# Row transposes issued singly between the relus, two more units turned straight from SBUF, and weight splits that begin six units earlier, in a one-core kernel of attention and a mixture of experts

## The reference

```python
def ref(x, ...):                      # x: (4, 1024, 256) float32
    xn = layernorm(x)
    s = attention(xn)                 # 8 heads of 128, one shared K and V, causal; Wo at the end
    g = silu(moe(xn))                 # 8 experts, top 2 of a router, softmax gates
    return x + s * g

def moe(x):
    logits = x @ router_w + router_b
    gating = softmax(only_top_2(logits))
    h = relu(x @ w1[e] + b1[e])       # for each expert e: 256 -> 1024
    y = h @ w2[e] + b2[e]             # 1024 -> 256
    return sum over e of y * gating[:, e]
```

## Time and profile before

| | us |
|---|---|
| median of three runs | 1049.65 |
| lowest, highest | 1047.79, 1051.46 |
| the profiled execution | 1046.62 |
| its span, first to last instruction | 1044.80 |
| PE busy in the span | 983.1 (94%) |
| VectorE (DVE) busy | 856.7 (82%) |
| ScalarE (ACT) busy | 641.7 (61%) |
| GpSimd (POOL) busy | 333.9 (32%) |
| mean granted clock of PE | 0.997 of full speed |

### The profile page before, as it was taken

How to read it: one execution, slowest core, us unless ns; L and a number is a source line. 1 busy time by engine, 2 the same in 40 slices (tenths; PEclk the granted TensorE clock), 3 DMA queues, 4 the chain that set the end, 5 groups by cost and what they waited for, 6 DMA issues and landing times.

```text
span 1044.8 us, 25199 instructions
## 1 busy us (share of the span) xinstructions
PE 983.1 (94%) x8422; PEld 763.7 (73%) x8422; DVE 856.7 (82%) x1700; ACT 641.7 (61%) x1382; POOL 333.9 (32%) x342
## 2 busy tenths in 40 slices
PE   0798999999999999998999999999999999999997
PEld 0566888888888898885666667676776776777776
DVE  7895587787765546458999999999999999999972
ACT  3843332333332334336989889898888888888860
POOL 2014999899997300002101101212122111212111
PEclk9999999999999999999999999999999999999999
DMA  8978667778766522217999999999999999999993
GB/s 282 250 284 174 176 192 188 201 183 199 177 174 174 146 47 63 61 37 177 166 183 189 167 180 169 197 190 172 190 189 180 185 182 181 180 170 167 173 174 101
DMA packets 428269, 179.44 MB, mean 172 GB/s; under 512 B 363850, under 2 KB 417940, under 8 KB 427380
## 3 DMA queue, kind: packets, MB, share of 16 engines
q1 hardware_dynamic: 364416, 131.75, 61.6%
q10 hardware_dynamic: 57252, 28.38, 12.2%
q0 software_dynamic: 6480, 17.70, 7.3%
HBM read 54.94 MB, written 34.87 MB: 86 GB/s over the span
## 4 chain that ended last, share of the span: by engine, by line
PE 35%; DVE 14%; issue 2%; DMA 1%; ACT 1%; SPq 1%; DVEq 0%; ACTq 0%
PE b_psS L1376 11%; PE b_psO L1404 11%; PE b_psJ L1421 6%; DVE b_ph L1617 5%; PE b_psJ L1335 5%; DVE b_nmax L1579 4%; PE b_psS L1432 2%; PE b_psO L1407 1%; DVE b_outs L1623 1%; DVE b_psJ L1587 1%; DVE b_Q L1601 1%; DMA b_pT<-b_ph 1%; DVE b_psS L1577 0%; DVE b_f L1629 0%; ACT b_pr L1486 0%
## 5 line engine op out<-in xcount | busy, mean ns | idle before, releaser
L1036 PE MATMUL psU<-bxT,w_p 128*128 128x256 f16 (+1 forms) x1920 | 287.4, 261 | 9.0 <-DMA bxT<-expert_rows 3.0
L1127 ACT ACTIVATE h<-psU,bias 128x256 f32<-128x256 f32 (+1 forms) x320 | 123.7, 448 | 255.2 <-PE psU L1036 182.9
L1045 PE MATMUL psY<-w_p,hp 128*128 x1704 | 274.7, 274 | 0.6 <-DVE hp L1157 0.6
L1486 ACT ACTIVATE b_pr<-b_psS,b_nmax 128x1024 f32<-128x1024 f32 (+7 forms) x256 | 188.0, 742 | 55.5 <-DVE b_nmax L1577 36.0
L1376 PE MATMUL b_psS<-b_kp,b_Q 128*128 128x512 f16 (+3 forms) x1152 | 215.2, 326 | 2.6 <-PEq L1216 1.5
L1036 PEld LDWEIGHTS psU<-bxT,w_p 128*128 x1920 | 187.3, 98 | 31.9 <-issue 13.2
L1404 PE MATMUL b_psO<-b_pT,b_vp 128*128 128x256 f16 x1536 | 202.9, 273 | 5.2 <-issue 3.4
L1617 DVE SCALAR_TENSOR_TENSOR b_ph<-b_pr,b_rrec,b_ph 128x1024 f16<-128x1024 f32 (+7 forms) x256 | 199.1, 809 | 1.8 <-ACT b_ph L1516 1.8
L1155 DVE CAST hp<-h 128x512 f16<-128x512 f32 (+1 forms) x160 | 91.7, 573 | 126.7 <-ACT h L1127 112.6
L1516 ACT ACTIVATE b_ph<-b_pr,b_rrec 128x1024 f16<-128x1024 f32 (+7 forms) x256 | 187.9, 779 | 0.0
L1045 PEld LDWEIGHTS psY<-w_p,hp 128*128 128x128 f16 x1704 | 166.5, 98 | 22.2 <-issue 1.4
(11 more groups left out here) (197 smaller groups left out, 1060.2 us busy)
## 6 DMA issues: line engine op xcount, KB each, us to landing
wstage<-in_L_ffn_w SPq DMA_DIRECT2D x48, 256.0 KB
expert_rows<-rowx SPq DMA_DIRECT2D x67, 128.0 KB
expert_outputs<-y ACTq DMA_DIRECT2D x31, 256.0 KB
b_pT<-b_ph SPq DMA_TRANSPOSE x320
a_x_all<-in_L_attn_x SPq DMA_DIRECT2D x8, 512.0 KB, 8.9
a_w_raw<-in_L_ffn_w SPq DMA_DIRECT2D x4, 1024.0 KB, 9.1
xn_split<-a_xp SPq DMA_DIRECT2D x4, 1024.0 KB, 9.0
xn_turned<-a_xT SPq DMA_DIRECT2D x3, 1024.0 KB, 16.1
```

The lines of the kernel that those rows point to most:

```text
L1036: mm = eng.matmul(psU[w % U][:, g % 2, 0:tiles * P].rearrange("p (t r) -> p t r", t=tiles), weight(n, a * W1 + c * H + g * P, P), bxT[n % ...
L1045: mm = eng.matmul(psY[n % 2][:, t, :], hp[n % 2][:, a, g, t * P:(t + 1) * P], weight(n, 2 * W1 + (2 * g + b) * D, D), start=(g == 0 and k ...
L1127: a = eng.activation(h32[w % 4][:, g, 0:rows], psU[w % U][:, g, 0:rows], ACT.Relu, bias=bias[:, ds(e * HT + 2 * q + g, 1)], scale=1.0 / WS)
L1486: a = eng.activation(pr[k % 3][:, o:o + w], psS[BUF[i]][:, :, :].rearrange("p a n -> p (a n)")[:, o:o + w], ACT.Exp, bias=nmax[:, at:at + ...
```

## The change

- The number of units that are turned straight becomes six: 4 and 5 join. Their two row buffers lie in the second buffer of `hp`, which block 1 is the first to fill, so VectorE waits before its first split of block 1 for both transposes. The four ring buffers go on with unit 6. GpSimd's gathers of units 4 and 5 still wait for the straight transposes of 0 and 1.
- ScalarE's transposes: `load(n, t)` issues one. In block n the first one for block n + 2 stands between the second and the third relu pair, the second one (if that block is a twin) between the third and the fourth; the read of the number of expert n + 1 stands there too. The first waits for the stores of its unit, as before, and for the straight transposes of units 4 and 5.
- VectorE reads the expert's number for its addition at the block's start, before its first split.
- GpSimd gathers 4 and 5, and from unit 6 on alternates gather and split. SP, too, alternates store and load of weights from unit 6 on, and b2's broadcast stands before the store of unit 8.

```diff
--- before.py
+++ after.py
@@ -137,7 +137,9 @@
     moe = Arena(nc, late_at)
     wstage = [moe.take(f"wstage{i}", [P, 512], F32) for i in range(2)]
     pe16 = Arena(nc, moe.at).take("a_pe16", [P, 2, T], F16)
-    rowx = [moe.take(f"rowx{i}", [P, 2 * D], F16) for i in range(4)]
+    RING = 4
+    STRAIGHT = 6
+    rowx = [moe.take(f"rowx{i}", [P, 2 * D], F16) for i in range(RING)]
     bxT = [moe.take(f"bxT{i}", [P, 2, 2 * DC, P], F16) for i in range(3)]
     table_at = moe.at - 2 * 2 * 2 * DC * P * 2
...
     WQ, WO = E * PIECES, E * PIECES + 4
     ALL = WO + 4
 
+    def home(n):
+
+        return n if n < STRAIGHT else (n - STRAIGHT) % RING
+
+    def turn(n):
+
+        return 16 * (1 if n < STRAIGHT else 2 + (n - STRAIGHT) // RING)
+
     def gather(eng, n):
 
-        if n >= 4:
-            eng.wait_ge(st_[n % 4], 16 * (n // 4))
-        eng.indirect_dma_start(rowx[n % 4][:, :], None, xp_d, bass.IndirectOffsetOnAxis(ap=who[:, FLOW[n]:FLOW[n] + 1], axis=0)).then_inc(gx_[n % 4], 16)
+        if n >= STRAIGHT:
+            eng.wait_ge(st_[home(n)], turn(n) - 16)
+        elif n >= RING:
+            eng.wait_ge(st_[n - RING], 16)
+        eng.indirect_dma_start(rowx[home(n)][:, :], None, xp_d, bass.IndirectOffsetOnAxis(ap=who[:, FLOW[n]:FLOW[n] + 1], axis=0)).then_inc(gx_[home(n)], 16)
 
     def keep(eng, n):
 
-        eng.wait_ge(gx_[n % 4], 16 * (n // 4 + 1))
-        eng.dma_start(rows_d[n * P:(n + 1) * P, :], rowx[n % 4][:, :]).then_inc(st_[n % 4], 16)
+        eng.wait_ge(gx_[home(n)], turn(n))
+        eng.dma_start(rows_d[n * P:(n + 1) * P, :], rowx[home(n)][:, :]).then_inc(st_[home(n)], 16)
 
...
     def loaded(n):
 
-        return sum(16 * len(units_of(k)) for k in range(2, n + 1) if k % 3 == n % 3)
-
-    def load(eng, n):
-
-        if n >= 3:
+        return sum(16 * len(units_of(k)) for k in range(STRAIGHT // 2, n + 1) if k % 3 == n % 3)
+
+    def load(eng, n, t):
+
+        if t == 0:
             eng.wait_ge(eu_, 4 * (n - 3) + 4)
-        for t, m in enumerate(places_of(n)):
-            eng.wait_ge(st_[m % 4], 16 * (m // 4 + 1))
-            if m < 6:
-                eng.wait_ge(st_[m - 2], 16)
+            if n == 3:
+                for m in range(4, STRAIGHT):
+                    eng.wait_ge(st_[m], 16)
+        if t < len(units_of(n)):
+            m = places_of(n)[t]
+            eng.wait_ge(st_[home(m)], turn(m))
             eng.dma_start_transpose(bxT[n % 3][:, t], rows_d[m * P:(m + 1) * P, :]).then_inc(ld[n % 3], 16)
...
-    hp = [sb(f"hp{i}", [P, 2, HT, R], F16) for i in range(2)]
+    hp = [sb("hp0", [P, 2, HT, R], F16)]
+    hp1_at = area.at
+    hp.append(sb("hp1", [P, 2, HT, R], F16))
     assert area.at <= v["top_at"]
+    early_rows = Arena(v["nc"], hp1_at)
+    v["rowx"] += [early_rows.take(f"rowx{i}", [P, 2 * D], F16) for i in range(v["RING"], STRAIGHT)]
...
     def on_sync(eng):
-        for n in range(2, 4):
+        for n in range(2, STRAIGHT):
             v["straight"](eng, n)
-        for n in range(4, AHEAD):
-            v["keep"](eng, n)
-        eng.wait_ge(kvp_, len(KV))
-        eng.dma_start(b2b[:, :], b2.rearrange("e d -> (e d)").partition_broadcast(P)).then_inc(b_l, 16)
-        for n in range(AHEAD, AHEAD + 4):
-            v["keep"](eng, n)
         p = FIRST + 2
-        for n in range(AHEAD + 4, UNITS):
+        for n in range(STRAIGHT, UNITS):
+            if n == 8:
+                eng.wait_ge(kvp_, len(KV))
+                eng.dma_start(b2b[:, :], b2.rearrange("e d -> (e d)").partition_broadcast(P)).then_inc(b_l, 16)
             v["keep"](eng, n)
             if p < v["ALL"]:
                 v["stage"](eng, p)
@@ -1010,8 +1024,8 @@
                     eng.wait_ge(wd_, p - 1)
                 v["put_wo"](eng, p - 2 - v["WO"])
             p += 1
-        for j in range(4):
-            eng.wait_ge(st_[j], 16 * len(range(j, UNITS, 4)))
+        for n in range(UNITS - v["RING"], UNITS):
+            eng.wait_ge(st_[v["home"](n)], v["turn"](n))
         eng.wait_ge(wd_, v["ALL"])
         eng.wait_ge(v["wk_"], 64)
         for r in range(4):
@@ -1064,7 +1078,7 @@
             if n == 1:
                 eng.wait_ge(kvc_, len(KV))
             if n < NBLK:
-                if n < 2:
+                if n < STRAIGHT // 2:
                     eng.wait_ge(st_[2 * n], 16)
                     eng.wait_ge(st_[2 * n + 1], 16)
                 else:
...
         eng.wait_ge(v["own_"], 1)
+        ahead = expert(eng, 0)
         for n in range(NBLK):
-            e = expert(eng, n)
+            e = ahead
             rows = len(units_of(n)) * P
             for q in range(PAIR):
                 w = PAIR * n + q
+                if q in (2, 3) and STRAIGHT // 2 <= n + 2 < NBLK:
+                    v["load"](eng, n + 2, q - 2)
+                if q == 3 and n + 1 < NBLK:
+                    ahead = expert(eng, n + 1)
                 eng.wait_ge(up_, w + 1)
                 if w >= 4:
                     eng.wait_ge(hl_, w - 3)
@@ -1133,10 +1152,6 @@
                 eng.activation(kq(r)[0][:, 0], kq_t[:, :], ACT.Identity, bias=kq(r)[1]).then_inc(kqa_, 1)
             if n in KV_AT:
                 kv_high(KV_AT[n])
-            if n == 0:
-                v["load"](eng, 2)
-            if n + 3 < NBLK:
-                v["load"](eng, n + 3)
             if n >= 2:
                 store(n - 2)
             if n - 1 in KV_AT:
@@ -1152,12 +1167,14 @@
             eng.wait_ge(rl_, w + 1)
             sl, rows = slice(2 * q, 2 * q + 2), slice(0, len(units_of(n)) * P)
             full, hi, lo = h32[w % 4][:, :, rows], hp[n % 2][:, 0, sl, rows], hp[n % 2][:, 1, sl, rows]
+            if n == 1 and q == 0:
+                for m in range(v["RING"], STRAIGHT):
+                    eng.wait_ge(st_[m], 16)
             eng.tensor_copy(hi, full).then_inc(hh_, 1)
             eng.wait_ge(hh_, w + 1)
             eng.tensor_tensor(lo, full, hi, ALU.subtract).then_inc(hl_, 1)
...
-        def rows(n):
-            e = expert(eng, n)
+        def rows(n, e):
             if n == 0:
                 eng.wait_ge(b_l, 16)
             if n >= 3:
@@ -1177,9 +1194,11 @@
             v["first_low"](eng, q)
         eng.wait_ge(v["own_"], 1)
         for n in range(NBLK):
+            if n >= 2:
+                e = expert(eng, n - 2)
             for q in range(PAIR):
                 if q == 1 and n >= 2:
-                    rows(n - 2)
+                    rows(n - 2, e)
                 split(n, q)
                     eng.wait_ge(kqa_, r + 1)
                     eng.scalar_tensor_tensor(kq(r)[0][:, 1], kq_t[:, :], kq(r)[1], kq(r)[0][:, 0], ALU.add, ALU.subtract).then_inc(kqb_, 1)
-        rows(NBLK - 2)
-        rows(NBLK - 1)
+        for n in range(NBLK - 2, NBLK):
+            rows(n, expert(eng, n))
 
     def on_gpsimd(eng):
-        for n in range(4, AHEAD + 4):
+        eng.wait_ge(v["own_"], 1)
+        for n in range(4, STRAIGHT):
             v["gather"](eng, n)
         p = FIRST
         eng.wait_ge(wd_, FIRST)
         eng.wait_ge(v["xk_"], 48)
         eng.wait_ge(v["kqs_"], 16)
-        for n in range(AHEAD + 4, UNITS):
+        for n in range(STRAIGHT, UNITS):
             v["gather"](eng, n)
             if p < v["ALL"]:
                 v["split"](eng, p)
```

More of the change, by code:

```diff
@@ L168, in build @@
     wh0_ = whole.enter_context(nc.semaphore("first_w_high"))
-    gx_ = [whole.enter_context(nc.semaphore(f"x_gathered{i}")) for i in range(4)]
-    st_ = [whole.enter_context(nc.semaphore(f"x_kept{i}")) for i in range(4)]
+    gx_ = [whole.enter_context(nc.semaphore(f"x_gathered{i}")) for i in range(STRAIGHT)]
+    st_ = [whole.enter_context(nc.semaphore(f"x_kept{i}")) for i in range(STRAIGHT)]
     xs_ = whole.enter_context(nc.semaphore("xn_stored"))
@@ L184, in build @@
     KV_STORE = tuple(0 if r < 3 else 1 if r < 11 else 2 for r in range(len(KV)))
-    AHEAD = 8
     WQ, WO = E * PIECES, E * PIECES + 4
     ALL = WO + 4
+    def home(n):
+        return n if n < STRAIGHT else (n - STRAIGHT) % RING
+    def turn(n):
+        return 16 * (1 if n < STRAIGHT else 2 + (n - STRAIGHT) // RING)
     def gather(eng, n):
-        if n >= 4:
-            eng.wait_ge(st_[n % 4], 16 * (n // 4))
-        eng.indirect_dma_start(rowx[n % 4][:, :], None, xp_d, bass.IndirectOffsetOnAxis(ap=who[:, FLOW[n]:FLOW[n] + 1], axis=0)).then_inc(gx_[n % 4], 16)
+        if n >= STRAIGHT:
[3 more added lines that the diff above has]
+        eng.indirect_dma_start(rowx[home(n)][:, :], None, xp_d, bass.IndirectOffsetOnAxis(ap=who[:, FLOW[n]:FLOW[n] + 1], axis=0)).then_inc(gx_[home(n)], 16)
     def keep(eng, n):
-        eng.wait_ge(gx_[n % 4], 16 * (n // 4 + 1))
-        eng.dma_start(rows_d[n * P:(n + 1) * P, :], rowx[n % 4][:, :]).then_inc(st_[n % 4], 16)
+        eng.wait_ge(gx_[home(n)], turn(n))
+        eng.dma_start(rows_d[n * P:(n + 1) * P, :], rowx[home(n)][:, :]).then_inc(st_[home(n)], 16)
     def straight(eng, m):
@@ L964, in experts @@
```

(4 more changed lines are left out.)

## The result

The changed kernel took 1032.93 us, median of 4 runs (1031.27 to 1035.21), against 1050.18 before: ratio 0.9837, 95% interval [0.9811, 0.9863]. The forecast was 1039.1, its range ended at 1033.5. Two repeats, each beside new runs of the kernel before, gave 0.9888 [0.9865, 0.9912] and 0.9855 [0.9823, 0.9887], so the gain is 12 to 17 us. In the two repeats, 12 and 15 us, it lies inside the range of gains that the prediction allowed (3 to 16). Two executions further down stand apart, one of `r2_changed_again` (1729.13 us, mean granted clock 0.568) and one of `k2_loads_at_end` (1048.58); ratios and medians leave both out, and neither is explained.

The account below looks back on a forecast made before the run. PE was taken to bound the experts' stretch, with 16.5 us of excess to win. Terms 4.5 + 2.6 + 4.2 - 0.6 = 10.7, called 10.5, off the median 1049.65 gave 1039.1 us; range 1033.5 to 1046.5.

Parts of the forecast that it names:

- step 2: Blocks 3 to 22: transposes between the relus fit a twin block's slots; 2.6 of 3.8 us gained, 1.2 left for slow issues.
- step 3: Blocks 23 to 39: last relus still late behind single blocks, 0.4 us remaining per pair; 4.2 of 8.2 us gained.
- Step 1: Start: turning units 4 and 5 straight from SBUF removes PE's 3.02 us wait and the low clock; 4.5 us gained.
- Step 4: VectorE's read of the expert's number at the block's start helps its chain by some 0.4 us, counted within other steps.
- Step 5: Transposes issued one block later, lead about one and a half blocks, still over 10 us: no cost.
- Step 6: GpSimd's splits from unit 6 slow the gathers and thin the supply of rows at the start; cost 0.6 us.
- Step 7: Earlier splits make GpSimd wait 3 to 8 us at piece 48 for the K/V stores; no effect on the time.
- Step 8: b2's broadcast is issued some 3 us later but lands before block 0's rows are added; cost nothing, or up to 1 us.
- B: Nearly all 16.5 us go, if VectorE has slack where 0.4 was counted: 1034 us; chance 5%.
- A: Start: b2's broadcast delays unit 8's row and stops PE; cost 2 to 5 us, 1041 to 1044; chance 20%.
- C: Twin blocks beside splits: VectorE's operations behind the last relu each wait out a GpSimd operation; 1055 us; chance 8%.
- D: PE's waits return in single blocks at 1 us each, start loses half; gain under 3, 1047 to 1049; chance 5%.

Follow-up runs that it names:

- r2_changed_again: The changed kernel run again as it is, beside new runs of the kernel before: ratio 0.9855.
- k2_loads_at_end: The changed kernel with ScalarE's two transposes back behind a block's last relu, numbers still read ahead: 1034.27 us, ratio 0.9869.
- e5: The kernel before with only GpSimd's splits moved to begin at unit 6: 1044.49 us, ratio 0.9988.
- e6: The changed kernel without straight units 4 and 5 and with VectorE reading the number late: 1039.13 us, ratio 0.9927.
- e1: The kernel before with only ScalarE's transposes and number reads moved between the relus, splits from unit 12: 1042.26 us, ratio 0.9943.
- k1: The changed kernel with ScalarE reading the expert's number at each block's start again, transposes still between the relus: 1031.90 us, ratio 0.9846.
- e7: The changed kernel with VectorE reading the expert's number between its first and second bank again: 1031.52 us, ratio 0.9858.
- e4: The changed kernel with GpSimd gathering units 6 to 11 in a row and splits from unit 12: 1041.58 us, ratio 0.9937.

## Why the prediction was wrong

The sign and the places were right, the size was 6.2 us short. **What failed are the losses that steps 2 and 3 left standing: 1.2 and 4.0 us.** Measured: nothing is left of the first (-0.6), and of the second 2.4, all of it in blocks 23 to 26; the 0.4 a pair that made up most of it measured 0.06. Both steps added the relus and the issues on ScalarE's queue one behind the other, and step 2 kept its 1.2 for slow issues. The runs show that a transpose issue lies beside its relu pair, and that a relu which comes up to 1 us late is made up by the slack behind it.

The account in numbers: between the medians 17.2 went, the forecast had 10.5. (The forecast missed by 6.2 and not by 6.7, because a fourth run of the kernel before raised its median by 0.5.) By the traces 14.0 of excess went, 3.5 more than forecast; 2.6 came back (PE's entry 1.1, attention 1.5, neither of them the change's); the other 5.8 is how the two profiled executions stand to their medians (3.6 below and 2.3 above), of which no trace shows a cause. That 17.2 is more than the 16.5 which the prediction called all that can be won comes from this last part alone. So the runs explain 3.5 of the miss, and the rest is spread between executions.

- **Step 1** (start, 4.5). 3.7 in this pair, 4.3 to 4.6 in the two repeats: right. But the straight units aren't the only cure: e5 and e6 keep the old way with splits from unit 6 and lost only 1.7 and 1.3, without a wait for the turned rows. The traces point at the broadcast of b2, which was not tested by itself. Before and in e1, where PE stopped 3.02 and 3.72 for these rows, it was issued at 89.53 and 90.53, within 0.4 us of the second of their transposes (89.92 and 90.27), it landed at 99.47 and 102.91, and PE's wait ended at 101.67 and 104.19. In e5 and e6 the loads of weights in front push it to 94.12 and 93.62, 4 us behind the second transpose (89.96 and 89.43). Gathers and stores from unit 8 on come later there too, so the broadcast alone isn't shown to be it.
- **Step 2** (blocks 3 to 22, 2.6 gained, 1.2 left for slow issues). 4.4 gained, nothing left. The sum for the last slot, "0.84 + 1.29 + 0.73", is one behind the other, but ScalarE's queue works ahead of its engine:

```profile
332.36 0.47 ACT L1146 ACTIVATE h<-psU,bias 128x256 f32<-128x256 f32 x1 [1.13 <-PE psU L1050]
332.56 1.42 ACTq L245 DMA_TRANSPOSE bxT<-expert_rows  x1
332.73 0.47 ACT L1146 ACTIVATE h<-psU,bias 128x256 f32<-128x256 f32 x1
334.33 0.47 ACT L1146 ACTIVATE h<-psU,bias 128x256 f32<-128x256 f32 x1 [1.13 <-PE psU L1050]
334.46 1.21 ACTq L245 DMA_TRANSPOSE bxT<-expert_rows  x1
334.70 0.47 ACT L1146 ACTIVATE h<-psU,bias 128x256 f32<-128x256 f32 x1
336.40 0.47 ACT L1146 ACTIVATE h<-psU,bias 128x256 f32<-128x256 f32 x1 [1.24 <-PE psU L1050]
```

  The transpose is issued 0.20 after the pair's first relu has begun, and the second relu starts inside it. A pair with its transpose takes 0.20 + 1.42 instead of 2.13. The rows of before had it: the transpose at 285.16 begins 0.19 after the relu at 284.97. Slow issues did come and cost nothing that stayed: the issue of 2.37 at 107.77 ended at 110.14, the read followed, and block 2's last relu came at 110.87, 0.6 late; block 3 made up these 0.6. In block 4 an issue of 2.71 made the last relu 1.0 late, and block 5 made that up.
- **Step 3** (blocks 23 to 39, 4.2 gained, 4.0 left). 5.8 gained, 2.4 left. The same sum: the fourth relu came 0.11 late (idle 1.24 instead of 1.13), not 1.1, and a pair keeps 0.06 us, not 0.4. (By its own terms, 1.1 + 0.84 + 0.2 + 0.42 + 0.69 against 2.95, the step gives 0.3 a pair; 0.4 was rounded up.) The read is not what is hidden. From the end of the issue at 335.67 to the fourth relu lie 0.73, the read's full time; the slot holds 0.13 + 1.21 + 0.73 = 2.07 against a bank every 1.965. What is hidden is the relu pair. In its old place (k1) the read stands behind a store's issue of 0.35 to 0.38 instead of a transpose, and fits.
- **Step 4**: no worth shows (e7), against 0.4.
- **Step 5** right: no wait for a transpose of unit 6 or later.
- **Step 6 failed in kind.** It priced the early splits at -0.6, a risk with no use (the start lost 0.8, -0.1 and 0.2 in three traces). They are what lets the rest of the gain through: with splits from 12, e4 loses 10.4 at block 18. The step counted the supply of rows and never asked when TensorE wants which expert; the slack of 0.09 could be read from before. That the forecast of a gain survives this error is luck: the change happened to contain this part.
- **Step 7** right: GpSimd stood 5.48 for the K/V stores at piece 48 (3 to 8 was said), and still had 3.4 in hand at block 18. The second row is the eighth piece of expert 6, done 3.4 before block 17's last relu:

```profile
231.89 0.66 POOL L291 TENSOR_SCALAR wstage<-wstage 128x512 f32<-128x512 f32 x1 [5.48 <-DMA later_kv<-a_kv_o]
...
262.95 1.16 POOL L295 TENSOR_TENSOR w_p<-wstage,w_p 128x512 f16<-128x512 f32 x1
```

- **Step 8** right in effect: the broadcast was issued at 94.27, 4.7 later and not 3, but landed at 100.08, and nobody waited for it.

Of the rivals, B (5%) came nearest in time, 1034 against 1032.93; by the traces 14.0 of the 16.5 went, which is what the prediction's last sentence had as "nearer 14". Its condition, a hidden read, isn't what happened (step 3), and B's, slack where 0.4 was counted, is. A didn't come: unit 8's row, gathered at 93.22, was stored at 97.43, not 106. Nor were the DMA engines busier. From 85 to 100 their share was 0.87 before and 0.73 after; in e4, which lost nothing at the start, they were at 0.93, so their share doesn't decide either. The busy times of that stretch in the kernel before, the changed one and e4:

```profile
85.00:100.00 15.00, 13.65 (x124) 11.77 (x122) 6.64 (x12) 5.37 (x15) 5.33 (x6) 1.00 0.87 184
```

```profile
85.00:100.00 15.00, 14.59 (x133) 12.67 (x132) 13.48 (x14) 6.09 (x15) 13.82 (x16) 1.00 0.73 194
```

```profile
85.00:100.00 15.00, 15.00 (x139) 13.31 (x138) 8.95 (x16) 5.87 (x14) 5.63 (x7) 1.00 0.93 182
```

C and D didn't come. The second and third row show C's mechanism all the same, at the start: with splits VectorE needed 13.48 us for 14 operations, without them 8.95 for 16, so 0.96 against 0.56 each (the same casts and subtractions, 128x512), and PE stopped 0.4 for `hp` at 94. The Trainium skill (SBUF — State Buffer, section "SBUF: two separate sides") says that of VectorE and GpSimd the one that loses the shared port pair is blocked for the other's whole instruction; the rows agree that sharing costs VectorE dearly (they don't show how it is shared), and in steady blocks it stayed within VectorE's slack (excess -0.6 in blocks 3 to 17).

## What to carry to other kernels

Before a stop of the bound engine is removed, list every other thing that this engine waits for later, with its due time and when it is ready now; a slack of 0.1 us says that the gain ends there, and the part of a change that looks like a mere risk may be what moves that time. Costs on a queue that feeds a slack don't add: here one half alone was free, the other cost about 2 us, and both together 6 to 11 (on another chip), so a part is judged by whether the sum passes the slot. Instructions of a queue (DMA issues, register reads) are timed by when the next operation of the engine could start, not by adding durations.

## What the runs showed of the hardware

- In the rows of 332 to 337, ScalarE's transpose issues of 1.42 and 1.21 us begin 0.20 and 0.13 after a relu has started, and another relu starts within them. A read of the expert's number behind an issue isn't hidden so: the next relu came 0.73 after the issue's end.
- After a stop of 8.17 us PE was granted 0.50 of its clock for 4.2 us; this added 2.2 to the wait (10.4 in all).
- The same change gained 17, 12 and 15 us in three sets of runs, and blocks 19 to 26 cost from 0.9 to 7.3 us in different executions. In the worst of them ScalarE waited 5.32 for a signal of which the profile shows no sender, while PE's rows show no stop from 344 to 351.3. This is not explained.
